# Splitting the staged weights into more chunks, and moving routing work of an attention and expert block

## The reference

```
xn  = layernorm(x)                                   # per row, 256 columns
q, k, v = split(xn @ wqkv.T)                         # 16 heads of 64
q, k = rope(rmsnorm(q) * q_w), rope(rmsnorm(k) * k_w)
att = softmax(causal(q @ k.T / 8)) @ v               # per head, 512 x 512
e   = argmax(xn @ gate_w.T)                          # one of 8 experts for each row
out = x + att @ wo.T + xn + xn @ expert_w[e].T
```

## Time and profile before

| what | value |
|---|---|
| median of 3 runs | 1976.66 us (1975.61 to 1977.33) |
| profiled execution, its own time | 1976.26 us |
| its span in the trace | 1974.3 us |
| PE busy | 1925.1 us, 98% |
| DVE busy | 1719.8 us, 87% |
| ACT busy | 1608.1 us, 81% |
| POOL busy | 1384.6 us, 70% |
| mean DMA rate | 74 GB/s |
| DVE's scaling of probabilities (L1142), mean of 512 | 0.527 us |

### The profile page before, as it was taken

The page is one execution under the profiler, slowest core; times in us unless marked ns, Lnnn a source line. Parts: engine busy times, 40 slices in busy tenths (PEclk is TensorE's granted clock), DMA queues, the critical chain, the costliest instruction groups (busy, mean ns, idle before and its releaser), DMA issues.

```text
span 1974.3 us, 51278 instructions
## 1 busy us (share of the span) xinstructions
PE 1925.1 (98%) x17288; PEld 1678.8 (85%) x17288; DVE 1719.8 (87%) x3936; ACT 1608.1 (81%) x5095; POOL 1384.6 (70%) x2023
## 2 busy tenths in 40 slices
PE   5999999999999999999999999999999999999996
PEld 5888888888888888888888888888888888888885
DVE  6988888898898888888988888888889888898875
ACT  4888888888888888888888888888888888888774
POOL 7877766677756877667775687766777578766753
PEclk8999999999999999999999999999999999999998
DMA  6110211212211132111331122212222112221344
GB/s 209 60 55 20 71 60 52 63 47 79 92 65 50 46 95 92 53 46 55 97 96 51 60 71 75 78 49 66 71 70 86 56 55 71 69 88 50 102 142 145
DMA packets 84561, 145.98 MB, mean 74 GB/s; under 512 B 9808, under 2 KB 63184, under 8 KB 84176
## 3 DMA queue, kind: packets, MB, share of 16 engines
q1 hardware_dynamic: 78160, 125.93, 19.8%
q0 software_dynamic: 6144, 16.79, 2.7%
HBM read 102.05 MB, written 40.63 MB: 72 GB/s over the span
## 4 chain that ended last, share of the span: by engine, by line
PE 91%; DVE 5%; issue 2%; POOL 1%; ACT 1%; DMA 1%; DVEq 0%; POOLq 0%
PE ps_g L814 41%; PE ps_g L936 14%; PE ps_g L947 13%; PE ps_s L895 10%; PE ps_g L876 6%; PE ps_g L895 2%; PE ps_s L890 2%; DVE neg_max L1130 2%; PE ps_g L890 1%; PE ps_g L841 1%; DVE prob L1142 1%; PE ps_g L823 1%; DVE ln_stat L1015 0%; POOL xn L578 0%; ACT prob L680 0%
## 5 line engine op out<-in xcount | busy, mean ns | idle before, releaser
L548 POOL TENSOR_TENSOR qk_rot<-qk_cos,qk_sin 128x128 f32<-128x128 f32 x1024 | 443.2, 464 | 482.0 <-PE ps_g L876 426.2
L814 PE MATMUL ps_g<-w_qkv,xn_t 128*128 128x384 f32 (+1 forms) x3072 | 636.2, 350 | 7.8 <-DVE w_qkv L1240 4.8
L814 PEld LDWEIGHTS ps_g<-w_qkv,xn_t 128*128 128x128 f32 x3072 | 523.2, 190 | 31.8 <-issue 22.6
L554 POOL TENSOR_TENSOR rms_inv<-ss,neg_half 128x8 f32<-128x8 f32 x256 | 425.2, 1661 | 0.0
L680 ACT ACTIVATE prob<-ps_s,neg_max 128x512 f32<-128x512 f32 (+2 forms) x768 | 417.5, 567 | 0.1
L688 ACT ACTIVATE prob_t<-ps_g 128x512 f32<-128x512 f32 (+2 forms) x768 | 394.1, 535 | 14.9 <-PE ps_g L936 13.3
L936 PE MATMUL ps_g<-ident,prob 128*128 128x128 f32 x2560 | 367.2, 274 | 13.6 <-DVE prob L1142 5.3
L559 POOL TENSOR_TENSOR qk_rot<-qk_rot,rms_inv 128x256 f32<-128x256 f32 x512 | 319.1, 644 | 20.1
L936 PEld LDWEIGHTS ps_g<-ident,prob 128*128 128x128 f32 x2560 | 300.6, 141 | 29.9 <-DVE prob L1142 14.5
L947 PE MATMUL ps_g<-prob_t,v 128*64 128x512 f32 (+3 forms) x2048 | 305.6, 441 | 3.2 <-ACT prob_t L688 2.3
L1130 DVE TENSOR_REDUCE neg_max<-ps_s 128x2 f32<-128x1024 f32 (+2 forms) x384 | 308.5, 860 | 0.0
(11 more groups left out here) (118 smaller groups left out, 3044.3 us busy)
## 6 DMA issues: line engine op xcount, KB each, us to landing
w_tile<-w_dram SPq DMA_DIRECT2D x120, 512.0 KB, 3.4
x_rows_s<-x_dram SPq DMA_DIRECT2D x120, 128.0 KB, 2.0
y_dram<-y_rows_s SPq DMA_DIRECT2D x120, 128.0 KB, 1.7
xin<-in_x SPq DMA_DIRECT2D x16, 512.0 KB, 4.1
out<-acc SPq DMA_DIRECT2D x15, 512.0 KB, 2.9
w_dram<-w_tile SPq DMA_DIRECT2D x8, 512.0 KB, 2.9
x_dram<-xn SPq DMA_DIRECT2D x2, 1920.0 KB, 18.9
y_back<-in_expert_t SPq DMA_DIRECT2D x8, 256.0 KB, 4.1
```

The costliest lines, as they stand in the source:

```text
L548: r = pool.tensor_tensor(rot[:, :, a, :], cos[:, :, a, :], sin[:, :, 1 - a, :], ALU.add)
L554: pool.tensor_tensor(rms_inv[:, ts[0]:ts[-1] + 1, :], ss[:, ts[0]:ts[-1] + 1, :], neg_half[:, :, :], ALU.pow).then_inc(s_pool_self, 1)
L814: r = pe.matmul(ps, lhs(a, c), rhs(b, c), start=(c == parts[0] and (a, b) == TERMS[0]), stop=(c == parts[-1] and (a, b) == TERMS[-1]))
```

## The change

The QKV weights are cut at pairs 0, 1, 2, 4 and 6, so there are ten chunks instead of six: two of 392 columns, two of 384 (pair 1), and six of 768. Chunks 2 and 3 are split right behind the transposed x of the first batch, ahead of the loop. Chunks 4 and 5 stay at the end of unit -1. Chunks 6 to 9 are split one in each of units 0 to 3, on ACT at the start of the unit and on DVE after the row maxima. PE's waits on `s_w_free` follow the new cuts. The staging buffers change with them; chunk 9 reuses the place of chunk 6 and is loaded in unit 1 of SP. SP's first loads are in another order: the first two expert weights come ahead of the zeroing of the scatter buffer, and so do chunks 6 to 8.

`find_tiles` is cut in two. DVE keeps the first two instructions as `find_passed`, now in the same unit as `find_slots`. POOL sums the eight flags by three additions, limits the result and converts it, five instructions that wait for each other, after its `start_rows` of that unit (for the last group two units later than DVE's part, in unit 122).

The rows of the last group are scattered three, three and two in units 120, 121 and 122. The gathers of batches 12 and 13 move one unit earlier (units 123, 124 and 126, 127 in place of 124, 125 and 127, 128), and so does the addition of batch 12 (124 and 125).

```diff
@@ -158,7 +158,7 @@
         s_masks_pe = sem("s_masks_pe")
-        w_loaded = [sem(f"w_loaded{i}") for i in range(6)]
+        w_loaded = [sem(f"w_loaded{i}") for i in range(10)]
         s_w_free = sem("s_w_free")
@@ -193,6 +193,7 @@
         s_slots = sem("s_slots")
+        s_passed = sem("s_passed")
         s_tiles = sem("s_tiles")
@@ -274,7 +275,7 @@
                 g, half = divmod(b, GROUP)
-                if u == (U + half if g == G - 1 else g * GROUP * PAIRS + (29 if g < G - 2 else 28) + 3 * half):
+                if u == (U + half if g == G - 1 else g * GROUP * PAIRS + (29 if g < G - 2 else 27) + 3 * half):
                     return b
@@ -282,7 +283,7 @@
                 g, half = divmod(b, GROUP)
-                last = U + 1 + half if g == G - 1 else min(U, g * GROUP * PAIRS + (31 if g < G - 2 else 30) + 3 * half)
+                last = U + 1 + half if g == G - 1 else min(U, g * GROUP * PAIRS + (31 if g < G - 2 else 29) + 3 * half)
                 if u == last:
@@ -380,10 +381,10 @@
                     return g, range(3 * n, min(3 * n + 3, GT))
-            for n in range(2):
+            for n in range(3):
                 g = slots_in(u - n)
                 if g == G - 1:
-                    return g, range(NT * n, NT * n + NT)
+                    return g, range(3 * n, min(3 * n + 3, GT))
             return None
@@ -409,13 +410,18 @@
+        STAGES = (0, 1, 2, 4, 6, PAIRS)
         staged = (prob_t[:, :, :, :].rearrange("p a t n -> p (a t n)"), prob[:, :, :].rearrange("p h n -> p (h n)"),
-                  acc[:, 0:2, :, :].rearrange("p a t c -> p (a t c)"))
+                  acc[:, 1, :, :].rearrange("p t c -> p (t c)"), x_rows_s[:, :, :].rearrange("p i c -> p (i c)"),
+                  xn[:, 1, 1:, :].rearrange("p t c -> p (t c)"))
-            stop = (0, E + 3 * PW, E + PAIRS * 3 * PW // 2, E + PAIRS * 3 * PW)
-            places = ((0, 0), (0, stop[1]), (0, 2 * stop[1]), (0, stop[1] + stop[2]), (1, 0), (2, 0))
+            stop = [E * (p > 0) + p * 3 * PW for p in STAGES]
+            one, two = stop[1], 3 * PW
+            places = ((0, 0), (0, one), (0, 2 * one), (0, 2 * one + two), (1, 0), (1, 2 * two),
+                      (2, 0), (3, 0), (4, 0), (2, 0))
             for n, (to, at) in enumerate(places):
@@ -427,19 +433,23 @@
             sp.dma_start(xin[:, :, :], x_rows[0]).then_inc(s_x_first, 16)
-            for n, (dst, src, raw) in enumerate(weight_chunks()):
-                if n == 2:
-                    for dst, table in ((nw[:, :, :], norm_w), (t_cos[:, :, 0, :], rope_cos), (t_sin[:, :, 0, :], rope_sin)):
-                        sp.dma_start(dst, table).then_inc(s_consts_pool, 16)
-                sp.dma_start(raw, src).then_inc(w_loaded[n], 16)
+            def load_weights(chunks):
+                for n in chunks:
+                    dst, src, raw = tuple(weight_chunks())[n]
+                    sp.dma_start(raw, src).then_inc(w_loaded[n], 16)
+            load_weights(range(0, 2))
+            for dst, table in ((nw[:, :, :], norm_w), (t_cos[:, :, 0, :], rope_cos), (t_sin[:, :, 0, :], rope_sin)):
+                sp.dma_start(dst, table).then_inc(s_consts_pool, 16)
+            load_weights(range(2, 6))
             sp.dma_start(wo_raw, wo_t).then_inc(s_wo_loaded, 16)
+            for e in range(2):
+                sp.dma_start(we_raw[:, e, :, :], expert_t[:, :, e, :]).then_inc(s_we_loaded[e], 16)
+            load_weights(range(6, 9))
             sp.wait_ge(s_x_zero, 1)
...
                              xn[:, 1, 0:1, :].to_broadcast([P, NS, C])).then_inc(s_zeroed, 16)
-            for e in range(2):
-                sp.dma_start(we_raw[:, e, :, :], expert_t[:, :, e, :]).then_inc(s_we_loaded[e], 16)
@@ -465,6 +475,9 @@
             def unit(u):
+                if u == 1:
+                    sp.wait_ge(s_w_free, 7)
+                    load_weights(range(9, 10))
                 if 0 <= u < E:
@@ -476,6 +489,7 @@
                 if u == E + 2:
+                    sp.wait_ge(s_w_free, 10)
                     for i in range(DEPTH):
@@ -586,6 +600,18 @@
+            def find_tiles(g):
+                def own(r):
+                    r.then_inc(s_pool_self, 1)
+                    pool.wait_ge(s_pool_self, seen(s_pool_self))
+                pool.wait_ge(s_passed, g + 1)
+                for n in (4, 2, 1):
+                    own(pool.tensor_tensor(passed[:, :, 0:n], passed[:, :, 0:n], passed[:, :, n:2 * n], ALU.add))
+                own(pool.tensor_scalar(tile_expert[:, :], passed[:, :, 0], float(E - 1), None, ALU.min))
+                pool.tensor_copy(tile_expert_i[:, g % 2, :], tile_expert[:, :]).then_inc(s_tiles, 1)
             def start_rows(b, half):
@@ -593,8 +619,8 @@
                     pool.wait_ge(s_xn_pe, b + 1)
-                if b < 4 and half == 0:
-                    pool.wait_ge(s_w_free, 6)
+                if b == 1 and half == 0:
+                    pool.wait_ge(s_w_free, 10)
                 pool.tensor_tensor(acc[:, b % 4, rows, :], xin[:, rows, :], xn[:, b % GROUP, rows, :], ALU.add)\
@@ -616,6 +642,9 @@
                     start_rows(batch_of(u), pair_of(u))
+                found = ranks_in(u - 3) if u >= U - PAIRS else ranks_in(u - 2)
+                if found is not None:
+                    find_tiles(found)
                 if live(u + 2):
@@ -726,6 +755,8 @@
                     scale_probs(u - 1, 3)
+                if 0 <= u < 4:
+                    high_weights(6 + u)
                 if 0 <= u < E:
@@ -744,9 +775,6 @@
                     softmax(u, 3)
-                if u == -1:
-                    high_weights(2)
-                    high_weights(3)
                 if live(u + 2) and not turns_x(u):
@@ -793,6 +821,8 @@
             take_xt(0)
+            high_weights(2)
+            high_weights(3)
             for u in units:
@@ -828,8 +858,8 @@
                     pe.wait_ge(s_xt_lo, NC * (b + 1))
-                if u in (1, PAIRS // 2) and t == 0:
-                    pe.wait_ge(s_w_free, 4 if u == 1 else 6)
+                if u in STAGES[1:-1] and t == 0:
+                    pe.wait_ge(s_w_free, 2 * STAGES.index(u) + 2)
                 n = NT * u + t
@@ -1064,6 +1094,8 @@
                 dve.wait_ge(s_rank_taken, g + 1)
+                if g >= 1:
+                    dve.wait_ge(s_tiles, g)
                 own(dve.tensor_tensor(filled[:, :, :], rank[:, GT, :].unsqueeze(2).to_broadcast([P, E, GT]),
@@ -1079,14 +1111,11 @@
-            def find_tiles(g):
+            def find_passed(g):
                 own(dve.tensor_tensor(end_tile[:, :], first_tile[:, :], tiles_of_e[:, :], ALU.add))
-                own(dve.tensor_tensor(passed[:, :, :], tile_no[:, :].unsqueeze(2).to_broadcast([P, NS, E]),
-                                      end_tile[:, :].unsqueeze(1).to_broadcast([P, NS, E]), ALU.is_ge))
-                own(dve.tensor_reduce(tile_expert[:, :], passed[:, :, :], AX.X, ALU.add))
-                own(dve.tensor_scalar(tile_expert[:, :], tile_expert[:, :], float(E - 1), None, ALU.min))
-                dve.tensor_copy(tile_expert_i[:, g % 2, :], tile_expert[:, :]).then_inc(s_tiles, 1)
+                dve.tensor_tensor(passed[:, :, :], tile_no[:, :].unsqueeze(2).to_broadcast([P, NS, E]),
+                                  end_tile[:, :].unsqueeze(1).to_broadcast([P, NS, E]), ALU.is_ge).then_inc(s_passed, 1)
@@ -1174,9 +1203,8 @@
                     take_xt(batch_of(u) + 1)
-                if u == -1:
-                    low_weights(2)
-                    low_weights(3)
+                if 0 <= u < 4:
+                    low_weights(6 + u)
                 if live(u) and batch_of(u) + 1 < B:
@@ -1195,13 +1223,12 @@
                     find_slots(G - 1)
-                    find_tiles(G - 1)
+                    find_passed(G - 1)
                 elif slots_in(u) is not None and slots_in(u) < G - 1:
                     find_slots(slots_in(u))
+                    find_passed(slots_in(u))
                 if ranks_in(u - 1) is not None and ranks_in(u - 1) < G - 1:
                     find_first(ranks_in(u - 1))
-                if slots_in(u - 1) is not None and slots_in(u - 1) < G - 1:
-                    find_tiles(slots_in(u - 1))
                 if live(u):
@@ -1247,6 +1274,8 @@
             take_xt(0)
+            low_weights(2)
+            low_weights(3)
             dve.wait_ge(s_iota_dve, 1)
```

## The result

The changed kernel takes 1962.47 us (median of 4 runs, 1961.97 to 1963.07) against 1976.61 (1975.61 to 1977.33) for the kernel before on the same chip: a ratio of 0.9929, 95% interval [0.9912, 0.9946]. The gain is 14.1 us where 8 were forecast, and 1962.47 lies 0.3 us under the range. Two of the four runs lie under its lower end of 1962.8 and two above it. The profiled execution's span is 1960.3 us in place of 1974.3.

What follows compares the result with a forecast made beforehand. PE, busy 98% of the span, was taken to bound the kernel between its two ends, with POOL's gathers pacing the end. Gains of 1.0 + 3.15 + 1.3 + 2.5 = 7.95 us from 1976.26 gave 1968.3 us, range 1962.8 to 1972.8.

Steps and rivals of the forecast that it cites:

- Middle: Units where DVE runs `find_tiles`: moving it removes 3.65 us of PE waits, 0.5 given back; 3.15 us gained.
- Last group: Units 120 to 122: 0.6 us from fewer DVE routing instructions, 0.7 from unit 121's PE wait; together 1.3 us.
- Front: Start through unit 3: less weight splitting before unit 0 gains 3.4 us, units 1 to 3 give back 2.4; net 1.0.
- the clock holds: Rival for the first units: PE keeps full clock after the shorter third stall, 2.3 us less, 1966.0 us; chance 0.22.
- End: After PE's last tile: eight gathers left instead of ten, so the last lands 2.5 us earlier.
- Costed at nothing: Loads, added waits, POOL's five small instructions and SP's later last-group fetch: all covered by slack, 0 us.
- The slower rival: Slots units: POOL's small instructions hold DVE's scalings, 1.66 us of PE for each of seven groups; 1979.9 us, chance 0.04.

Runs made afterwards that it cites:

- doses: The changed kernel with 2 to 12 small dependent DVE additions, writing an unused tile, ahead of the first scaling in one unit of each sixteen; 1958.55 us.
- only_weights: The kernel before with the ten weight chunks alone; span 1971.7 us.
- only_tiles: The kernel before with `find_tiles` cut into DVE's two instructions and POOL's five, nothing else changed; span 1966.5 us.
- gap32_out: The kernel after with 32 unused bytes a partition just ahead of the attention output `o_t`; 1957.34 us.
- xn_t_off: The kernel after with 32 unused bytes a partition ahead of the rotary work tiles, and `xn_t` alone moved 32 bytes past a multiple of 64; 1962.51 us.

## Why the prediction was off

- **Middle: the step that failed.** "So they go: 4.1 - 1.36 + 0.91 = 3.65 us for seven groups" took the shown waits for the whole price of the stalls. What the runs show in its place: the seven units became shorter by 1.46, 0.84, 0.81, 0.81, 0.99, 1.19 and 0.85, together 6.95 us: 3.30 more than the waits, 0.47 for each of seven stalls, which is what doses measured apart at the same place. Given back were 0.50 in unit 9, 0.12 to 0.15 in each of six later units and 0.38 in unit 45, together 1.7 and not 0.5 (the 0.2 that are left to 5.45 lie in steps too small to name). Unit 45's is no price of the tiles: only_weights has it too, with `find_tiles` still on DVE. That unit takes 14.44 us there, as its like in the other groups (units 29 and 61) do in the kernel before; the 14.04 of the kernel before is the odd value, and why is open.
- **Last group: the same error.** In unit 120 0.70 us came (0.6 forecast, and there a shorter stall remained, so no 0.47). In unit 121 2.32 came: the whole wait of 1.66 and 0.66 behind it, where 0.7 was taken. That DVE's scalings were 3.91 us long beside POOL's addition and rotation holds: with those moved 1.3 us forward, the same scalings take 1.19, and in only_tiles they are long again where they meet in unit 120 (3.46).
- **Front: the sizes were near, and the clock was luck.** I took the clock's second fall as staying; in the profiled execution it held, so the rival "the clock holds" came true there. From the first transposed probabilities to the next scores it is 5.98 us and not 7.62, so in this pair it is worth 1.64 and not 2.3. The rest of the front was near: 3.12 gained up to there (3.4 forecast, 2.87 us of stall left), and 1.76 given back in units 1 to 3 (2.4). 3.12 + 1.64 - 1.76 = 3.0. In seven of eleven executions with this front the clock did fall, at a price of 0.6 to 1.0 us. So both branches occur with this kernel. What failed in this term is its form: one branch taken whole, with the length of the half clock read from a single execution. The 3.0 us are a lucky pair as well: unit 4 starts at 89.05 in the kernel after, the earliest of those eleven (to 89.89, mean 89.52), and at 92.05 in the kernel before, the latest of four executions with its front (from 91.12, mean 91.62). By the means the front is worth some 2.1 us against 1.0 forecast.
- **End: right.** Eight gathers, 2 × 1.25 us, the last landing still the end of the chain; 2.5 us as forecast.
- **Costed at nothing, and nothing:** loads, the added waits, POOL's five small instructions, SP's later fetch of the last group (it went out at 1855.85, and PE didn't wait). The slower rival, that POOL's instructions hold DVE's scalings, didn't occur: in each of the seven slots units DVE's pairs of scalings take 0.88 and 0.75 us. The Trainium skill (GPSIMD Engine Reference, Specifications) says that GpSimd shares its SBUF interfaces with VectorE and that it contends with VectorE where the latter runs in a two-port mode or has two SBUF inputs. The prediction drew from it that more small instructions would mean more such meetings. These traces show long scalings only beside POOL's addition and rotations, as in unit 121, and none beside the five small instructions.
- Together: 2.0 us too little at the front, 2.3 in the middle, 1.8 in the last group, none at the end: 6.05 of the 14.0 us that the span lost. With the front at its mean of 2.1 the largest error left is the hidden part of PE's stalls, in the middle and in the last group.

## What to carry to other kernels

A wait of a pipelined engine as a profile shows it need not be what its removal brings; here 0.47 us came on top at one place, 0.66 at another and next to nothing at a third. Date the same instruction in each iteration instead, and compare the stalled iteration with one that isn't. Where the clock falls behind a stall in one execution and not in the next, give both outcomes, price them by rows at either level, and look at several executions before a difference is put down to the change. And keep an experiment's scratch tile out of its control: add the same tile to both.

## What wasn't expected of the hardware

- A PE stall shown as 0.16 to 0.91 us, ahead of the four transposes in the middle of a unit, costs some 0.47 us beyond its shown wait (doses; the seven units of the middle).
- Around a PE stall of 2.36 us the granted clock fell to half in one execution (gap32_out), and around one of 2.37 us it held in another (xn_t_off), though the two kernels differ up to there in the place of some tiles only.
- 32 unused bytes a partition changed the time by 6 us of 1962 (0.3%). 4.9 us of it lie in the output projections' 1536 matmuls (212.4 us busy against 207.5); 64 bytes changed nothing.
- Two changes to the last group's routing each made unit 121 shorter by the same 2.32 us when made alone. One of them alone made the unit before longer by 1.16 us, since a DVE scaling there took 3.13 us beside POOL's addition and rotations; the pair didn't.
